# Three pairs on VectorE and two blocks on TensorE in the last sweep's softmax sums, in place of two pairs and four blocks

## The reference, cut to what matters

```python
# stage 0, "plain": 8 heads
sim = jnp.einsum('bihd,bjhd->bhij', q, k) * SCALE
attn = jax.nn.softmax(sim, axis=-1)
out = jnp.einsum('bhij,bjhd->bihd', attn, v).reshape(B, N, INNER)
return out @ Wo + bo
# stage 3, "biased": 16 heads
scores = jnp.einsum('bhqd,bhkd->bhqk', q, k) * D_MODEL ** (-0.5) + attn_bias
weights = jax.nn.softmax(scores, axis=-1)
out = jnp.einsum('bhqk,bhkd->bhqd', weights, v)   # then heads side by side, @ Wp.T
```

## Time and profile before

| | |
|---|---|
| median of 3 executions | 1891.12 us (1890.51 to 1895.9) |
| profiled execution, its own time | 1889.08 us |
| its span from first to last instruction | 1887.3 us |
| TensorE busy | 1821.0 us, 96% |
| VectorE busy | 1543.2 us, 82% |
| ScalarE / GpSimd busy | 863.7 us / 926.7 us |
| mean granted TensorE clock | 0.981 of full speed |
| last sweep, plain, TensorE's first weighing to its last sum | 504.1 to 529.45 us of the span |
| last sweep, biased, the same | 1759.4 to 1784.75 us of the span |

### The profile page before, as it was taken

One profiled execution on the slowest core, in us unless ns is written; L12 is line 12 of the kernel. 1 busy time (PEld: TensorE's weight loads), 2 busy tenths in 40 slices (PEclk: granted clock), 3 DMA queues, 4 the chain that ended last, 5 costly groups with the idle time before them and its releaser, 6 DMA issues. The chain is left out here.

```text
span 1887.3 us, 45395 instructions
## 1 busy us (share of the span) xinstructions
PE 1821.0 (96%) x17913; PEld 1241.3 (66%) x17913; DVE 1543.2 (82%) x2141; ACT 863.7 (46%) x1210; POOL 926.7 (49%) x438
## 2 busy tenths in 40 slices
PE   8999999999888899999999999999999999999788
PEld 5667666766657688666676667666766676667545
DVE  5666766676877676899999999999999999999784
ACT  4666666666643454243434344434443444343402
POOL 0356655665652153065475547554755475547300
PEclk9999999999989799999999999999999999999889
DMA  3000110000030141000000000120000000000100
GB/s 143 10 15 0 51 67 14 0 14 10 7 142 3 55 167 50 13 10 15 14 0 14 14 14 0 48 70 14 0 14 14 13 1 14 14 8 2 35 17 12
DMA packets 27778, 52.64 MB, mean 28 GB/s; under 512 B 4260, under 2 KB 15285, under 8 KB 27189
## 3 DMA queue, kind: packets, MB, share of 16 engines
q1 hardware_dynamic: 27232, 51.34, 8.3%
q10 hardware_dynamic: 468, 0.16, 0.0%
HBM read 50.97 MB, written 0.52 MB: 27 GB/s over the span
## 5 line engine op out<-in xcount | busy, mean ns | idle before, releaser
L390 POOL TENSOR_TENSOR biased_sums<-biased_sums,biased_scores 128x1024 f32<-128x1024 f32 x216 | 512.5, 2372 | 138.7 <-ACT biased_scores L699 119.2
L767 DVE TENSOR_TENSOR biased_scores<-ps,bias 128x1024 f32<-128x1024 f32 x256 | 311.1, 1215 | 34.7 <-PE ps L478 33.4
L781 DVE TENSOR_TENSOR ps<-ps,biased_scores 128x512 f32<-128x512 f32 x480 | 332.0, 692 | 4.1
L788 DVE TENSOR_TENSOR biased_scores<-biased_scores,ps 128x1024 f32<-128x1024 f32 x256 | 305.1, 1211 | 4.1 <-PE ps L536 3.4
L699 ACT ACTIVATE biased_scores<-biased_scores 128x1024 f32<-128x1024 f32 x256 | 262.9, 1052 | 98.1 <-DVE biased_scores L788 95.9
L390 POOL TENSOR_TENSOR plain_sums<-plain_sums,plain_scores 128x1024 f32<-128x1024 f32 x104 | 246.5, 2370 | 60.7 <-ACT plain_scores L699 50.3
L781 DVE TENSOR_TENSOR ps<-ps,plain_scores 128x512 f32<-128x512 f32 x240 | 167.4, 697 | 118.1 <-ACT plain_scores L682 113.7
L478 PE MATMUL ps<-biased_queries,keys_again 64*128 64x256 f32 x2048 | 257.2, 390 | 6.2 <-DVE biased_scores L767 5.5
L490 PE MATMUL ps<-biased_scores,values_again 128*64 128x256 f32 x2048 | 245.4, 382 | 3.5 <-ACT biased_scores L699 3.2
L425 PE MATMUL ps<-weights_again,context_again 128*64 128x128 f32 x4000 | 243.4, 275 | 0.0
L425 PEld LDWEIGHTS ps<-weights_again,context_again 128*64 128x64 f32 x4000 | 224.0, 138 | 27.3 <-issue 16.5
(11 more groups left out here) (423 smaller groups left out, 2202.9 us busy)
## 6 DMA issues: line engine op xcount, KB each, us to landing
moe_w<-in_moe_w SPq DMA_DIRECT2D x32, 256.0 KB, 2.8
weights_again<-in_wqkv SPq DMA_DIRECT2D x45, 128.0 KB, 2.1
context<-in_ctx_t SPq DMA_DIRECT2D x4, 1024.0 KB, 6.5
context_again<-in_ctx_t SPq DMA_DIRECT2D x4, 1024.0 KB, 7.4
bias<-in_fside SPq DMA_DIRECT2D x1, 4096.0 KB, 13.4
biased_w_out<-in_w_out SPq DMA_DIRECT2D x16, 256.0 KB, 2.6
context<-in_ctx_t SPq DMA_DIRECT2D x2, 1536.0 KB, 8.8
context_again<-in_ctx_t SPq DMA_DIRECT2D x2, 1536.0 KB, 9.9
```

The lines of the kernel that those rows point to most:

```text
L390: pool.tensor_tensor(both(SUM[:, :, :, :]), both((E[:, 0] if kp == 1 else SUM)[:, :, :, :]), both(E[:, kp, :, :, :]), ALU.add).then_inc(su ...
L767: dve.tensor_tensor(E[:, kp, :, :, :].rearrange("p (h t) n j -> p h t (n j)", h=2), scores_bank(kp).rearrange("p (h t n) -> p h t n", h=2, ...
L781: ins = dve.tensor_tensor(to, highest, E[:, kp, :, n, :], ALU.max)
L788: dve.tensor_tensor(at, at, c.ps[:, LOWER, :].rearrange("p (a j) -> p a j", a=HQ).unsqueeze(2) .to_broadcast([P, HQ, 2, P]), ALU.add).then ...
```

## The change

`LATE_SUMS` goes from 12 to 10, so TensorE's `add_up` takes blocks 8 and 9 only, and the blocks 10 to 15 are summed by VectorE in three pairs: (10, 11), (12, 13) and (14, 15). A third buffer is needed, another piece of `KT`. At the end TensorE turns three pairs instead of two, and the two projections stand behind the second and the third turn, no longer behind the first and second.

```diff
-    LAST_SUMS, LATE_SUMS = 8, 12
+    LAST_SUMS, LATE_SUMS = 8, 10
+    LATE_PAIRS = (NP - LATE_SUMS) // 2
...
-        LATE = (PEAKS_BOTH, KT[:, 0:2 * HQ * P].rearrange("p (n a j) -> p n a j", n=2, a=HQ))
+        LATE = [PEAKS_BOTH] + [KT[:, n * 2 * HQ * P:(n + 1) * 2 * HQ * P].rearrange("p (n a j) -> p n a j", n=2, a=HQ)
+                               for n in range(LATE_PAIRS - 1)]
...
                 def sums_out_last(m):
-                    for j in range(2):
+                    for j in range(LATE_PAIRS):
                         pe.wait_ge(late_summed, j + 1)
                         for n in range(2):
                             turn_sums(LATE[j][:, n, :, :], False, False)
-                        project_head(m, j, False)
+                        if j > 0:
+                            project_head(m, j - 1, False)
...
                 def sum_late(m):
-                    for j in range(2):
+                    for j in range(LATE_PAIRS):
                         kp = LATE_SUMS + 2 * j
                         dve.wait_ge(exp_done, NP * m + kp + 2)
```

## The result

Over 18 executions each, the changed kernel took 1896.34 us in the median and the kernel before 1891.36 us; the ratio is 1.0021, with a 95% interval of 1.0014 to 1.0028, so 4.0 us slower by the ratio (0.0021 x 1891.36); the two medians alone differ by 5.0 us. That is less than 0.3%, as forecast, but more than the +0.74 us of the sum. A second comparison, 12 executions against 35, gave 1894.66 against 1892.88 us, ratio 1.0004 (0.9994 to 1.0014), or +0.8 us. Both are within 0.3%. The first is slower beyond its interval, the second is not; together the intervals run from -1 to +5 us.

What follows compares the result with a forecast made beforehand. TensorE was taken to bound the end of each last sweep, with VectorE having room. Plain +0.36 and biased +0.38 us give +0.74 us: profiled 1889.08 becomes 1889.8, median 1891.12 becomes 1891.9; range 1889.0 to 1895.5 us.

Steps and rivals of the forecast that it cites:

- the sum: Both cross-attentions' last sweeps together: plain +0.36 us and biased +0.38 us, making +0.74 us.
- The forecast's own upper bound: Whole-kernel median if waits cost up to 2.4 us more in all: 1891.12 + 0.74 + 2.4 = 1894.3 us.
- The new wait on `late_summed`: TensorE, before the first turn of the tail, waits for VectorE's first add: 1.17 of the 1.94 us are lost.
- The first add: VectorE in the last sweep: again 3.22 us long beside GpSimd's add, ending at 523.76 as before.
- A turn: TensorE's 16 matmuls for one more pair in the last sweep's tail: 0.92 us added.
- The row of two turns: First two turns with no projection between: a 0.92 us turn, then another 0.21 us waiting for the second buffer.
- the tail of 4.86 us: Plain last sweep from 524.95: turn, projection, turn, projection and sum take 4.86 us, ending at 529.81 instead of 529.45.
- Rival B: TensorE's clock falls in the new wait: slower, 3.2 to 11.6 us on top of the forecast; chance 5%.
- the weighing by idle time alone: Clock-fall argument at the tail: new waits of 1.17 and 0.21 us behind 7 us of unbroken work speak against a fall.
- B's own yardstick: TensorE idle time and the clock: 2.3 us before 498.21 left it at 1.00, 2.50 us brought a fall.
- Rival A: VectorE's first add is not held up and runs in 1.21 us: faster by up to 2.1 us; chance 7%.
- Rival C: The program does something else at its seams, such as where a stage ends: a few us, either sign; chance 5%.

Runs made afterwards that it cites:

- experiment 10: Kernel before with one redundant turn of the first pair's buffer behind the real one, no wait for an add; 1896.88 against 1892.52 us, ratio 1.0014.
- experiment 9: Changed kernel with each turn of the last sweeps multiplying by 32 columns of ones instead of one; 1889.83 us, ratio 0.9986 to the kernel before.
- experiment 3: Changed kernel with the projections back behind the first and second turn, run twice; ratios 0.9995 and 0.9998 to the kernel before.
- experiment 8: Changed kernel reordered: GpSimd's sum, first pair, projection, second and third pair, second projection last; 1888.67 us, ratio 0.9977 to the kernel before.
- experiment 4: Changed kernel with GpSimd's sum turned first, in the place of the wait; 1887.95 us, ratio 0.9985 to the kernel before.
- experiment 7: Changed kernel reordered: GpSimd's sum, projection, first pair, projection, second and third pair; 1887.79 us, ratio 0.9976 to the kernel before.
- experiment 11: Changed kernel: GpSimd's sum, first pair, projection, last two pairs, second projection last, 32 columns in last-sweep turns; 1886.84 us, ratio 0.9966 to before.
- experiment 6: Changed kernel with five unread wide matmuls of a weighing filling the wait for the first add; 1894.67 us, ratio 1.0017 to the kernel before.

## Why the prediction was right, and where its step failed

**The direction and the class were right**: slower, by less than 0.3%. The ratio 1.0021 on the 1891.12 us that stood in the profile section gives 1895.1, at the upper edge of 1889.0 to 1895.5. The changed kernel's own median, 1896.34 us, lies above that range, and the likeliest value, 1891.9, was too low: the measured +4.0 us is over five times the +0.74 us of the sum. The forecast's own upper bound was 1894.3; that the range holds 1895.1 is owed to the 1.2 us added for the spread of executions, and is luck as far as the clock goes. The second comparison (+0.8 us) is near the sum, but its interval also holds no change at all.

**The mechanism that I costed is what happened.** The new wait on `late_summed`: 1.15 and 1.20 us at the weight load, 1.17 forecast. The first add: 3.21 and 3.26 us, not 1.21, so it was held up as before. A turn: 0.92 forecast, and 0.92 is what one more turn added in the plain tail of experiment 10. The row of two turns: 1.14 us from one to the next, 1.13 forecast (0.92 + 0.21). With the clock up, the whole change costs 5.91 - 5.69 = 0.22 us a sweep (experiment 9), and 0 with the projections left where they were (experiment 3: 5.68), where +0.36 and +0.38 were forecast; the tail of 4.86 us that I built from differences of weight loads was 0.14 us too long. One reason is in the rows: before, a turn's weight load ran 0.21 us ahead of its matmul (524.59 and 524.80), and the sum carries that lead along, but behind a wait both start together (526.65 in the changed kernel).

**The term that was mis-sized is the clock**, put at nothing in the sum. Rival B had 5%, and its outcome is what both profiles of the changed kernel show in all four tails, though not by B's way: the clock did not fall in the new wait but 1.6 to 4.3 us after it, with TensorE at work. The step that failed is the weighing by idle time alone ("The new waits are 1.17 and 0.21 us, behind 7 us of unbroken work, so the rows speak against it"). With the whole wait and the projections early the clock held 4 times of 4, and it fell without any wait in experiments 8 and 10, and with 0.2 us of one in experiment 4. What TensorE had done before each fall was turns, with at most one projection between them and 0.3 us of a second. With a projection behind each of the first two turns, or both behind the two, it held, and so it did with 32 columns in each turn. I had taken rows of TensorE without gaps for unbroken work, though the old rows already said that a turn multiplies single columns (128x1 in the earlier trace rows).

B's own yardstick, "that 2.3 us of it were harmless and 2.5 us were not", holds for the execution it was read from and not for the kernel. The same two waits, 2.29 us before the peaks are turned and 2.50 us before the first weighing, stand in the same code in every profile. In the changed kernel's first the clock was at 0.50 by 497.60, before the shorter one was over at 498.05, and in that of experiment 7 it held through both:

```profile
497.00:523.00 26.00, 21.22 (x230) 12.89 (x230) 24.83 (x26) 17.07 (x17) 16.65 (x7) 1.00 0.04 11
```

B's price was about right: 1.6 to 5.8 us a sweep, where the tails show 9.60 - 5.91 = 3.7, 1.8, 1.8 and 1.3 us.

**Behind the tail the times move too.** The tail is not the end of the matter, because the clock falls behind it in most profiles and the next stage begins at what it finds. I measured from the first add's end to the first matmuls of `delta_w` in the stage behind the plain one, and from the biased stage's first add's end to the last stage's first statistics, in us:

| kernel | plain | biased |
|---|---|---|
| before, two profiles | 14.7, 14.6 | 75.1, 74.8 |
| changed, two profiles | 17.4, 15.8 | 77.4, 77.7 |
| projections early, two profiles | 14.7, 13.6 | 75.1, 77.1 |
| mixed (experiment 7) | 12.6 | 74.1 |
| changed, 32 columns (9) | 13.8 | 75.0 |
| mixed, projection last, 32 columns (11) | 11.5 | 72.9 |

The changed kernel is +2.7 and +1.2 us in the plain stage, less than the tails' +3.9 and +2.1, so part of that loss comes back, and +2.3 to +2.9 in the biased one. Together that is +5 and +4 us in the two profiled executions, beside +4.0 in the first comparison of timed runs and +0.8 in the second. But the second profile with projections early has +2 us in the biased stage with no fall in its tail, so one profile by itself does not tell such a difference. Experiments 7, 9 and 11 gain behind the tail: 2.9, 0.8 and 5.2 us by this table against the mean of before, where their tails give 1.8, -0.4 and 1.8. (Experiment 11 gives 0.8 us of it back in the last stage, 33.9 us long in place of 33.1.) In experiment 11 the clock stayed up behind both tails for the 10 us shown, where in the profile of before it was at 0.50 from 532 on:

```profile
530.00:540.00 10.00, 7.26 (x29) 3.36 (x29) 5.40 (x19) 3.46 (x4) 0.00 (x0) 1.00 0.62 192
1786.00:1796.00 10.00, 6.63 (x46) 3.72 (x46) 6.53 (x21) 4.72 (x8) 0.29 (x1) 1.00 0.57 211
```

**Rival A** did not occur: the first add was held up every time. **Rival C** cannot be separated from the spread: the executions of before differ by 7.7 to 10.2 us within one comparison, in good part with their mean clock (about 1 us for each 0.001 of it in the runs of before).

**What stays open.** Why the clock fell at 528.2 in one execution and at 529.4 in another, and in only one of two tails in experiments 6, 8 and 10: the rows show that it can fall there, not when. How often it fell in the executions without a profile, and with it whether the second comparison's smaller difference is luck. The 1 to 2 us that experiments 7, 9 and 11 gained beyond the table above: the mean clock over all executions was 0.981 to 0.983 in them against 0.979 before, so the clock was low for less time, but one profile each does not show where. The 32 columns were not tried on the kernel before, and in experiments 9 and 11 they also stand in the direct sums ahead of the tail, which were not widened by themselves.

## What to carry to other kernels

Count a stretch of TensorE by what it multiplies, not by its busy share: a row of single-column matmuls in which every gap is filled can leave the granted clock at half, and then the wide matmuls behind it pay. Before moving work to another engine, ask what kind of work stands next to it now; in the profiles here the clock held in 4 of 4 tails with a projection behind each of the first two turns and in 0 of 4 with the two turns in a row, and the 16 matmuls fewer a sweep bought nothing by themselves (experiment 3). If the work must be thin, widening it where the instruction takes no longer, or putting wide work between, is cheap. Do not read a clock rule off one execution: the same wait in the same code had the clock fall in one and not in another. And when an add relieves the busy engine of work, check that the result is ready when that engine comes to it: of the 1.94 us that the removal was worth by the old rows, 1.15 to 1.20 us went straight into a new wait.

## What the runs showed of the hardware

A turn's matmuls took nearly the same time with 1 and with 32 moving columns (1.05 and 1.07 us for 32 rows), and the same kernel with 32 columns ran 0.9986 of before where with 1 column it had run 1.0021 and 1.0004. VectorE's add of two SBUF blocks took 3.20 to 3.26 us beside GpSimd's add in every profile and 1.21 us behind it; in the Trainium skill, "SBUF — State Buffer", section "Who interferes with whom", the two exclude each other and issue order decides, and the traces agree with that: VectorE's add, issued second, ended about one add's length after GpSimd's. The Trainium skill, "TensorE: Matmul & The Clock Gate", section "HAM oscillation — how this bites in real kernels", puts the clock's falls down to idle gaps; the runs here show a fall without any gap too, in experiment 10.
